# Third attention of a Flamingo-style kernel: its norms placed among residual rows, its groups turned into other banks, and eight tiles of scores ahead of group 2

## The chip, the cores and the metric

The kernel runs on one core of one Trainium2 chip. The metric is the device time of one execution in microseconds. TensorE (PE), VectorE (DVE), ScalarE (ACT), GpSimd (POOL) and SyncE (SP, which here only issues DMAs) each work through their own list of instructions in order. They meet at semaphores. Everything is float32 or a split of it in two parts.

## The reference, cut to what matters

Eight stages follow one another on `x` of 2 x 1024 tokens by 256: an attention and a feed-forward stage in each of four layers. Each stage normalizes `x`, computes, and adds its result, times a gate, to `x`.

```
x = x + tanh(g_ffn[1]) * ffn1(layernorm(x))              # dense: 8 experts, gated
x = x + tanh(g_xattn[2]) * attn2(layernorm(x), ctx)      # one head of 16, 64 keys
x = x + tanh(g_ffn[2]) * ffn2(layernorm(x))              # top-1 routing to 8 experts

attn2:  q = (x Wq) wq_h + bq_h;  k, v the same from ctx, 16 wide
        p = softmax(where(mask, -1e9, q k^T / 4))
        out = tile(p v, 16 times) Wo
ffn2:   logits = x router^T;  chosen = argmax;  rows gathered per expert, two matmuls
```

## The kernel before, in words

A tile is 128 tokens; there are 16 (`NT`), in four groups of four (`NG`, `GROUP`). `xs` holds `x`, `lnx` its normalized form, `xT` the transposed form that TensorE multiplies. The order of the work of every engine is written out by hand. The semaphores count: `x_done` residual rows, `ln_done` normalized tiles, `tr_done` transposed groups, `xt_done` copied groups.

A norm has four steps. `next_stats` takes the statistics of a tile behind its residual row (VectorE). `norm_moments` aggregates them for a group (VectorE). `norm_rstd` computes 1/sqrt on ScalarE (two instructions). `norm_group` writes four tiles of `lnx` (VectorE). TensorE then turns the group into two PSUM banks (`turn`) and ScalarE copies these into `xT` (`copy`).

**End of the second feed-forward stage (ffn1).** Its result lies transposed in `xT`; TensorE turns it back (`back`, L1050), two tiles to a bank in the order `BACK`, and VectorE adds the rows to `xs` (L2013) with `next_stats` (L1719) and `norm_moments` (L1694) between. Behind tiles 3 and 6 VectorE still adds up the last two blocks (`add_up`, L1947), for which the last turns back wait.

**Third attention (attn2).** TensorE first folds the weights (`wh`, into `wqkv`, copied by ScalarE at L1544), makes keys and values (banks 6 and 7) which VectorE takes over at L2245 and L2247, runs 24 multiplications whose result nobody reads (`fill`, L695), and turns group 0 and 1 (L1214). The order then is: queries of group 0 and 1, turns 2 and 3, scores of tiles 0 to 7, queries 2 and 3, six fills, the probabilities turned (L1238), scores of tiles 8 to 15, values. A query is a product of 16 x 512 that ScalarE copies with its bias (L1634). `bound` on VectorE (L2220 to L2225) masks the scores and subtracts their maximum, `exps` on ScalarE (L1643) exponentiates, `heads` on VectorE (L2232, L2235) divides and spreads the result over 128 columns. A loop over the 16 tiles follows: TensorE transposes a tile (L1272), ScalarE copies it (L1667), TensorE projects it, VectorE adds the row to `xs` (L2262), with `next_stats` and `norm_moments` between. Then come 40 fills.

**Third feed-forward stage (ffn2).** VectorE normalizes all four groups (`norm`, L1702) and computes the lower parts of the first weights (L2147). ScalarE, in this order: upper part of weight piece 0 (L1556), `norm_rstd` of group 3, pieces 1 to 3, and then the copies of the turned groups (L1579). TensorE turns the groups (L706) and multiplies them with the router (`logits_step`); VectorE takes the maxima from L2064 on and builds the row lists for the gathers.

Of the kernel before, what the change touches and what calls it, by code (L numbers as in the profile page):

```python
# [7 lines left out]
ALU = mybir.AluOpType  # L8
# [9 lines left out]
P = 128  # L18
# [3 lines left out]
NT = T // P  # L22
# [48 lines left out]
def build(nc, a, out, subs):  # L71
    with ExitStack() as ctx:
# [3 lines left out]
        def sem(name):  # L76
            return ctx.enter_context(nc.semaphore(name))
# [100 lines left out]
        with ExitStack() as a0_mem:  # L178
# [76 lines left out]
        a2_w, a2_wc, a2_kv, a2_kvb, a2_mask, a2_pool, in_a2 = (sem(f"a2_{n}") for n in ("w", "wc", "kv", "kvb", "mask", "pool", "in"))  # L255
        a2_q, a2_qc, a2_s, a2_min, a2_max, a2_sub, a2_exp, a2_ptr, a2_pt, a2_av, a2_rs, a2_oh, a2_tr, a2_ot, a2_proj = (
            sem(f"a2_{n}") for n in ("q", "qc", "s", "min", "max", "sub", "exp", "ptr", "pt", "av", "rs", "oh", "tr", "ot", "proj"))
        A2_Q, A2_S, A2_PTR, A2_AV, A2_TR, A2_PROJ = (4, 5, 4, 5), (6, 7), (0, 5), (1, 3), (0, 6), (1, 2)

        SLOT = {"11": 0, "12": 1, "21": 2, "22": 3}  # L260
# [425 lines left out]
        def _(pe):  # L686
# [5 lines left out]
            def fill(bank, count):  # L692

                for _ in range(count):
                    pe.matmul(ps[:, bank, 0:2 * P], filler[:, 0:P], filler, start=True, stop=True)  # L695
# [492 lines left out]
            def attn2(n):  # L1188
# [13 lines left out]
                    for k in range(KD):  # L1202
                        last = mm(ps[:, 6, b * HD:(b + 1) * HD], ctxD[:, k, b, :, :], wqkv[:, 2, k, :], k == 0, k == KD - 1)
                last.then_inc(a2_kv, 1)
                pe.wait_ge(x_done, NT * n - 2)
                fill(0, 24)

                def turn(g):
                    pe.wait_ge(ln_done, NT * n + GROUP * (g + 1))
                    if g >= 2:  # L1210
                        pe.wait_ge(xt_done, NG * n + g - 1)
                    for t in range(GROUP):
                        for k in range(KD):
                            last = pe.transpose(ps[:, g % 2 * 2 + k, t * P:(t + 1) * P],  # L1214
                                                lnx[:, g * GROUP + t, k * P:(k + 1) * P], ident[:, :])
                    last.then_inc(tr_done, 1)

                def query(g):
                    pe.wait_ge(xt_done, NG * n + g + 1)
                    if g >= 2:  # L1220
                        pe.wait_ge(a2_qc, g - 1)
                    for k in range(KD):
                        last = mm(ps[0:HD, A2_Q[g], :], wqkv[:, 0, k, :], xT[:, k, g * GT:(g + 1) * GT], k == 0, k == KD - 1)
                    last.then_inc(a2_q, 1)

                def scores(h):
                    pe.wait_ge(a2_qc, 2 * (h + 1))
                    pe.wait_ge(a2_kvb, 3)
                    for t in range(TB):
                        i = h * TB + t  # L1230
                        last = mm(ps[:, A2_S[h], t * S2:(t + 1) * S2], qhT[:, i * P:(i + 1) * P], khT[:, h, :], True, True)
                    last.then_inc(a2_s, 1)
# [14 lines left out]
                    last.then_inc(a2_av, 1)  # L1247

                turn(0)
                turn(1)  # L1250
                query(0)
                query(1)
                turn(2)
                turn(3)
                scores(0)
                query(2)
                query(3)
                fill(3, 6)
                turn_probs(0)
# [3 lines left out]
                for i in range(NT + 1):  # L1263
# [9 lines left out]
                    if i > 0:  # L1273
# [3 lines left out]
                        if i == 1:  # L1277
                            pe.wait_ge(a2_mask, 1)
                        mm(ps[:, A2_PROJ[(i - 1) % 2], 0:D], ot8[:, (i - 1) % 2, :], wo8[:, :], True, True).then_inc(a2_proj, 1)
                fill(7, 40)  # L1280

            if "attn2" in N:
                attn2(N["attn2"])
# [9 lines left out]
        def _(act):  # L1293
# [26 lines left out]
            def norm_rstd(n, g):  # L1320
                group_rstd(norm_no(n, g), g)
# [130 lines left out]
            def ffn1(n):  # L1452
# [87 lines left out]
                high(2 * UNITS - 1, "22")  # L1540
                high(2 * UNITS - 1, "21")
                act.preload_act_table_set("natural_log_exp_and_others")
                act.wait_ge(a2_w, 1)
                act.activation(wqkv[:, :, :, :], ps[:, 6, 0:3 * KD * HD].rearrange("p (i k j) -> p i k j", i=3, k=KD), ACT.Copy).then_inc(a2_wc, 1)  # L1544
                for g in range(NG):
                    norm_rstd(n + 1, g)

            def moe(layer, n):
                name = f"ffn{layer}"
# [81 lines left out]
            def attn2(n):  # L1631
                def query(g):
                    act.wait_ge(a2_q, g + 1)
                    act.activation(qhT[:, g * GT:(g + 1) * GT], ps[0:HD, A2_Q[g], :], ACT.Identity, bias=bh[:, 0:1]).then_inc(a2_qc, 1)  # L1634

                def copy(g):
                    act.wait_ge(tr_done, NG * n + g + 1)
                    act.activation(xT[:, :, g * GT:(g + 1) * GT], ps[:, g % 2 * 2:g % 2 * 2 + 2, :], ACT.Copy).then_inc(xt_done, 1)

                def exps(h):  # L1640
                    act.wait_ge(a2_sub, h + 1)
                    tiles = slice(h * TB, (h + 1) * TB)
                    act.activation(sc[:, 0, tiles, :], sc[:, 0, tiles, :], ACT.Exp).then_inc(a2_exp, 1)  # L1643

                def probs(h):
                    act.wait_ge(a2_ptr, h + 1)
                    act.activation(pt[:, h * PAIRS // 2:(h + 1) * PAIRS // 2, :], ps[:, A2_PTR[h], :].rearrange("p (q t) -> p q t", q=PAIRS // 2),
                                   ACT.Copy).then_inc(a2_pt, 1)
                copy(0)
                copy(1)  # L1650
                query(0)
                query(1)
                copy(2)
                copy(3)
                query(2)
                exps(0)
                query(3)
                probs(0)
                for i in range(NT):
                    if i == 1:  # L1660
                        exps(1)
                    if i == 2:
                        probs(1)
                    act.wait_ge(a2_tr, i + 1)
                    if i >= 2:
                        act.wait_ge(a2_proj, i - 1)
                    act.activation(ot8[:, i % 2, :], ps[:, A2_TR[i % 2], 0:P], ACT.Copy).then_inc(a2_ot, 1)  # L1667
                    if i in (7, 11, 15):
                        norm_rstd(n + 1, (i - 7) // 4)

            if "attn2" in N:
                attn2(N["attn2"])
# [9 lines left out]
        def _(dve):  # L1682
# [13 lines left out]
            def norm_moments(n, g):  # L1696
                moments(g, NT + 2 * GROUP * (g + 1) if n == 1 else NT * (n + 1) + GROUP * (g + 1))
# [113 lines left out]
            def mha(layer, m, n):  # L1811
# [89 lines left out]
                if soon:  # L1901
                    dve.wait_ge(ln_done, NT * (n + 1) + 3 * GROUP)
                    norm_group(n + 1, NG - 1)

            def ffn1(n):

                def x_sum(i, tp):
# [101 lines left out]
                for i in range(NT):  # L2009
                    if i in (3, 6):  # L2010
                        add_up(2 * UNITS - 1, 1, i // 6)
                    dve.wait_ge(f_back, i // 2 + 1)
                    dve.scalar_tensor_tensor(out=xs[:, i, :], in0=ps[:, BACK[i // 2], i % 2 * D:(i % 2 + 1) * D], scalar=gates[:, 5:6], in1=xs[:, i, :],  # L2013
                                             op0=ALU.mult, op1=ALU.add).then_inc(x_done, 1)
                    if i > 0:
                        next_stats(n, i - 1)
                    if i in (4, 8, 12):
                        norm_moments(n + 1, i // 4 - 1)
                next_stats(n, NT - 1)
                norm_moments(n + 1, NG - 1)  # L2020

# [116 lines left out]
            def moe(layer, n):  # L2138
                name = f"ffn{layer}"
                nth, cap, items, tiles = MOE.index(layer), CAP[layer], ITEMS[layer], IR[layer] // P  # L2140
                if layer:
                    norm(n)

                def weights_lower(*pieces):
# [72 lines left out]
            def attn2(n):  # L2217
# [10 lines left out]
                def heads(h):  # L2228
# [5 lines left out]
                    for r in range(2):  # L2234
# [1 line left out]
                                          av[:, r, :, 0:HD].unsqueeze(2).to_broadcast([P, half, HC, HD]),  # L2236
                                          rs2[:, r, h * half:(h + 1) * half].unsqueeze(2).unsqueeze(3).to_broadcast([P, half, HC, HD]),
                                          ALU.mult).then_inc(a2_oh, 1)
                dve.wait_ge(zeroed, 1 + 16 * 3)
                norm_group(n, 0)  # L2240
                norm_group(n, 1)
                dve.wait_ge(in_a2, 48)
                dve.wait_ge(a2_pool, 3)
                dve.wait_ge(a2_kv, 1)
                dve.tensor_scalar(khT[:, :, :], ps[0:HD, 7, 0:P].rearrange("p (b s) -> p b s", b=B), bh[:, 1:2], 0.25, ALU.add, ALU.mult).then_inc(a2_kvb, 1)  # L2245
                for b in range(B):
                    dve.tensor_tensor(vh[:, b, 0:HD], ps[:, 6, b * HD:(b + 1) * HD], bvh[:, :], ALU.add).then_inc(a2_kvb, 1)  # L2247
                norm_group(n, 2)
                norm_group(n, 3)
                dve.wait_ge(in_mask, 16 * MASKS[2])  # L2250
                link(dve.tensor_scalar(bmask[:, 0:TB, :], mask8[:, :, :], 0.0, BIG, ALU.is_equal, ALU.mult))
                link(dve.tensor_scalar(bmask[:, 0:TB, :], bmask[:, 0:TB, :], MASKED[2], None, ALU.add))
# [5 lines left out]
                for i in range(NT):  # L2258
                    if i == 4:
                        heads(1)  # L2260
                    dve.wait_ge(a2_proj, i + 1)
                    dve.scalar_tensor_tensor(out=xs[:, i, :], in0=ps[:, A2_PROJ[i % 2], 0:D], scalar=gates[:, 2:3], in1=xs[:, i, :],  # L2262
                                             op0=ALU.mult, op1=ALU.add).then_inc(x_done, 1)
                    if i > 0:
                        next_stats(n, i - 1)
                    if i in (4, 8, 12):
                        norm_moments(n + 1, i // 4 - 1)
                next_stats(n, NT - 1)
                norm_moments(n + 1, NG - 1)

# [54 lines left out]
```

## Time and profile before

| | |
|---|---|
| time, median of 3 runs | 1987.97 us (1986.66 to 1992.17) |
| the profiled execution's own time | 1972.97 us |
| its span in the trace | 1971.2 us |
| TensorE busy | 1848.1 us (94%) |
| VectorE busy | 1402.6 us (71%) |
| ScalarE busy | 1094.5 us (56%) |
| mean granted TensorE clock | 0.972 |

The change touches the stretch from about 1424 to 1497 us of the trace, which is 4% of the span. Times in rows are microseconds from the start of the span. A granted clock of 1.00 is TensorE at 2.4 GHz, 0.50 is 1.2 GHz; a value between them is a stretch that had both.

### The profile page before, as it was taken

What the parts mean: (1) busy time and instruction counts of PE and PEld (TensorE: products, weight loads), DVE (VectorE), ACT (ScalarE), POOL (GpSimd) and SP (SyncE); (2) the same over time, 40 slices, a digit from 0 to 9 for tenths busy, and PEclk for the clock granted to TensorE, in tenths of its full rate; (3) what the DMA queues carried; (4) which work ended last, traced back from release to release, by engine and by line L of the source; (5) the groups of instructions that cost most, each with busy time, mean ns of one, the idle gap of its engine ahead of it and who ended that gap; (6) DMA issues with size and microseconds to landing.
All of it is one profiled execution on the core that took longest, in us unless ns stands there. A gap on an engine that the chain in (4) does not pass through costs nothing.

```text
span 1971.2 us, 34855 instructions
## 1 busy us (share of the span) xinstructions
PE 1848.1 (94%) x11498; PEld 1557.3 (79%) x11498; DVE 1402.6 (71%) x2375; ACT 1094.5 (56%) x2003; POOL 730.8 (37%) x754
## 2 busy tenths in 40 slices
PE   7889996999999999999999999999998997898993
PEld 5579995877888888888888888888767997686993
DVE  4767777678777777777777777777766664866664
ACT  5548883685545555555555555455424774573771
POOL 6023331556434344353443534434002232342231
PEclk9999998999999999999999999999989999899997
DMA  4246662001000000100000000031114551203544
GB/s 126 71 144 200 200 176 76 2 17 33 17 32 16 32 32 16 32 16 32 32 16 32 21 27 32 16 116 50 30 38 150 147 147 50 71 2 118 176 138 142
DMA packets 113578, 138.95 MB, mean 70 GB/s; under 512 B 15332, under 2 KB 101606, under 8 KB 113504
## 3 DMA queue, kind: packets, MB, share of 16 engines
q1 hardware_dynamic: 105952, 121.70, 20.2%
q0 software_dynamic: 7552, 16.24, 2.8%
q8 instruction: 49, 0.80, 0.2%
q14 instruction: 25, 0.20, 0.0%
HBM read 117.22 MB, written 24.90 MB: 72 GB/s over the span
## 4 chain that ended last, share of the span: by engine, by line
PE 80%; DVE 10%; ACT 4%; issue 3%; DMA 2%; ACTq 0%; DVEq 0%; SPq 0%; POOL 0%; POOLq 0%
PE ps L688 43%; PE ps L949 10%; PE ps L950 10%; PE ps L951 10%; PE ps L695 2%; PE ps L882 1%; ACT ps L1595 1%; DVE xs L1799 1%; ACT wsplit L1556 1%; DVE bn L1719 1%; DVE wsplit L2180 1%; DVE lnx L1702 1%; PE ps L1149 1%; PE ps L1108 1%; DVE h_lo L2161 1%
## 5 line engine op out<-in xcount | busy, mean ns | idle before, releaser
L688 PE MATMUL ps<-h_hi,wsplit 128*128 128x512 f32 (+3 forms) x2016 | 588.5, 350 | 1.8 <-DVE xT L1947 1.3
L688 PEld LDWEIGHTS ps<-h_hi,wsplit 128*128 128x128 f32 x2016 | 366.7, 188 | 48.7 <-DVE xT L1947 1.8
L688 PE MATMUL ps<-h_lo,wsplit 128*128 128x512 f32 (+3 forms) x1008 | 352.5, 350 | 0.0
L574 POOL TENSOR_TENSOR wsplit<-wraw,zero 128x256 fp32r<-128x256 f32 (+2 forms) x160 | 150.9, 960 | 497.0 <-PE ps L951 407.7
L1477 ACT ACTIVATE lnx<-ps 128x512 f32<-128x512 f32 x384 | 229.3, 598 | 106.3 <-PE ps L951 63.6
L688 PE MATMUL ps<-xTh,wsplit 128*128 128x256 f32 (+2 forms) x992 | 254.9, 311 | 8.0 <-DVE h_lo L2161 4.4
L1486 ACT ACTIVATE h_act<-h_act 128x512 f32<-128x512 f32 x192 | 120.9, 629 | 211.8 <-DVE h_act L1925 211.7
L1947 DVE TENSOR_TENSOR xT<-xT,ps 128x1024 f32<-128x1024 f32 x124 | 151.3, 1220 | 117.7 <-PE ps L688 117.7
L1490 ACT ACTIVATE h_hi<-ps 128x512 fp32r<-128x512 f32 x256 | 152.6, 596 | 142.1 <-PE ps L688 139.8
L2161 DVE TENSOR_TENSOR h_lo<-ps,h_hi 128x256 fp32r<-128x256 f32 (+2 forms) x248 | 117.7, 475 | 151.3 <-ACT h_hi L1599 150.1
L1934 DVE TENSOR_TENSOR ps<-h_act,ps 128x512 f32<-128x512 f32 x256 | 177.4, 693 | 44.3 <-PE ps L951 30.2
L688 PEld LDWEIGHTS ps<-h_lo,wsplit 128*128 128x128 f32 x1008 | 189.5, 188 | 22.7
L949 PE MATMUL ps<-xTh,wsplit 128*128 128x512 f32 x512 | 203.1, 397 | 0.7 <-DVE xTl L1917 0.4
L950 PE MATMUL ps<-xTl,wsplit 128*128 128x512 f32 x512 | 202.5, 396 | 0.0
L951 PE MATMUL ps<-xTh,wsplit 128*128 128x512 f32 x512 | 202.5, 395 | 0.0
L635 POOL DMA_INDIRECT y_tok<-xT,y_idx x78 | 87.9, 1126 | 297.3 <-DVE xT L2176 283.0
L688 PEld LDWEIGHTS ps<-xTh,wsplit 128*128 128x128 f32 x992 | 174.6, 188 | 16.0 <-DVE h_lo L2161 12.2
L1595 ACT ACTIVATE ps<-ps,b1c 128x256 f32<-128x256 f32 (+2 forms) x248 | 120.7, 487 | 101.6 <-PE ps L688 100.5
L1925 DVE TENSOR_TENSOR h_act<-ps,lnx 128x512 f32<-128x512 f32 x192 | 132.5, 690 | 61.8 <-PE ps L951 61.6
L1938 DVE TENSOR_TENSOR h_lo<-ps,h_hi 128x512 fp32r<-128x512 f32 x256 | 174.5, 682 | 0.0
L628 POOL DMA_INDIRECT xT<-x_tok,x_idx x78 | 91.5, 1173 | 199.7 <-DVE x_idx L2120 173.2
L949 PE MATMUL ps<-wsplit 128*128 128x512 f32 x384 | 151.0, 393 | 2.9 <-DVE ps L1925 1.5
(289 smaller groups left out, 3580.3 us busy)
## 6 DMA issues: line engine op xcount, KB each, us to landing
wraw<-in_L_w SPq DMA_DIRECT2D x124, 512.0 KB, 3.9
wraw<-in_L_ffn_Wg SPq DMA_DIRECT2D x32, 256.0 KB, 2.7
wraw<-in_L_ffn_Wu SPq DMA_DIRECT2D x32, 256.0 KB, 3.0
wraw<-in_L_ffn_Wd SPq DMA_DIRECT2D x32, 256.0 KB, 3.6
x_tok<-lnx SPq DMA_DIRECT2D x12, 512.0 KB, 4.1
lnx<-y_tok SPq DMA_DIRECT2D x12, 512.0 KB, 5.9
y_tok<-lnx SPq DMA_DIRECT2D x3, 2048.0 KB, 13.8
wat<-in_attn SPq DMA_DIRECT2D x16, 256.0 KB, 4.8
```

The lines of the kernel that those rows point to most:

```text
L574: return pool.tensor_tensor(out_, in_, zero[:, :].to_broadcast(shape), ALU.add)
L688: return pe.matmul(out_, lhsT, rhs, start=start, stop=stop)
L949: pe.matmul(o, w_hi, x_hi, start=fresh, stop=False, skip_group_check=True)
L950: pe.matmul(o, w_hi, x_lo, start=False, stop=False, skip_group_check=True)
L951: pe.matmul(o, w_lo, x_hi, start=False, stop=True, skip_group_check=True).then_inc(p_early if m == 0 and i in (2, 5) else p_up, 1)
L1477: act.activation(dst, ps[:, 3 * m + (1 if i == 2 else 2), :], ACT.Copy).then_inc(p_copy, 1)
L1490: act.activation(h_hi[:, SLOT[c], :], ps[:, H_BANK[c], :], ACT.Copy).then_inc(p_hi, 1)
L1595: act.activation(ps[:, f % 2, 0:cap], ps[:, f % 2, 0:cap], func, bias=b1c[:, layer, bass.ds(ex * FC + f, 1)]).then_inc(m_act, 1)
L1934: dve.tensor_tensor(bank, h_act[:, c in ("12", "21"), :], bank, ALU.mult).then_inc(p_h, 1)
L1938: dve.tensor_tensor(h_lo[:, SLOT[c], :], ps[:, H_BANK[c], :], h_hi[:, SLOT[c], :].bitcast(F32), ALU.subtract).then_inc(p_lo, 1)
L1947: dve.tensor_tensor(xT[:, :, blk], xT[:, :, blk], ps[:, 6:8, :], ALU.add).then_inc(p_y, 1)
L2161: dve.tensor_tensor(h_lo[:, f % 4, 0:cap], ps[:, f % 2, 0:cap], h_hi[:, f % 4, 0:cap].bitcast(F32), ALU.subtract).then_inc(f_lo, 1)
```

## The change

- `norm_group` of attn2's groups 0, 1 and 2 moves from behind all 16 residual rows of ffn1 to behind rows 5, 10 and 14. VectorE's take-over of keys and values moves to row 12 (`keys_of_attn2`). ScalarE computes `norm_rstd` of groups 0 and 1 ahead of the copy of the folded weights, that of group 3 behind attn2's second copy.
- The groups are turned into banks 4-5, 6-7, 0-1 and 2-3. Groups 0, 2 and 3 wait for the residual rows that empty these banks, group 1 for the keys and values.
- TensorE's wait for ffn1's rows and the 24 fills ahead of the first turn go.
- TensorE's order is now turn 0, query 0, turn 1, query 1, scores of tiles 0 to 7, turn 2, query 2, turn 3, query 3. ScalarE's follows it, and `exps(0)` stands ahead of the copy of group 3.
- `norm_group` of ffn2's groups 0, 1 and 2 moves into attn2's residual loop, behind rows 7, 11 and 15, with their `norm_rstd` one tile earlier on ScalarE. Only group 3 is normalized behind the loop.
- The 40 fills behind the loop become 10 and a wait for the last residual row.

```
+        A2_TURN = (4, 6, 0, 2)
...
-                pe.wait_ge(x_done, NT * n - 2)
-                fill(0, 24)
                 def turn(g):
                     pe.wait_ge(ln_done, NT * n + GROUP * (g + 1))
-                    if g >= 2:
-                        pe.wait_ge(xt_done, NG * n + g - 1)
+                    if g == 1:
+                        pe.wait_ge(a2_kvb, 3)
+                    else:
+                        pe.wait_ge(x_done, NT * (n - 1) + {0: 10, 2: 14, 3: 16}[g])
...
                 turn(0)
+                query(0)
                 turn(1)
-                query(0)
                 query(1)
+                scores(0)
                 turn(2)
+                query(2)
                 turn(3)
-                scores(0)
-                query(2)
                 query(3)
...
-                fill(7, 40)
+                fill(7, 10)
+                pe.wait_ge(x_done, NT * (n + 1))
...
+                norm_rstd(n + 1, 0)
+                norm_rstd(n + 1, 1)
                 act.wait_ge(a2_w, 1)
                 act.activation(wqkv[:, :, :, :], ...).then_inc(a2_wc, 1)
-                for g in range(NG):
-                    norm_rstd(n + 1, g)
+                norm_rstd(n + 1, 2)
...
                 copy(0)
+                query(0)
                 copy(1)
-                query(0)
+                norm_rstd(n, NG - 1)
                 query(1)
                 copy(2)
-                copy(3)
                 query(2)
                 exps(0)
+                copy(3)
                 query(3)
...
-                    if i in (7, 11, 15):
-                        norm_rstd(n + 1, (i - 7) // 4)
+                    if i in (6, 10, 14):
+                        norm_rstd(n + 1, (i - 6) // 4)
...
+            def keys_of_attn2():
+                dve.wait_ge(in_a2, 48)
+                dve.wait_ge(a2_pool, 3)
+                dve.wait_ge(a2_kv, 1)
+                dve.tensor_scalar(khT[:, :, :], ...).then_inc(a2_kvb, 1)
+                for b in range(B):
+                    dve.tensor_tensor(vh[:, b, 0:HD], ...).then_inc(a2_kvb, 1)
...
+                    if i == 5:
+                        dve.wait_ge(zeroed, 1 + 16 * 3)
+                    if i == 12:
+                        keys_of_attn2()
+                    if i in (5, 10, 14):
+                        norm_group(n + 1, (5, 10, 14).index(i))
...
-                if layer:
+                if layer == 2:
+                    norm_group(n, NG - 1)
+                elif layer == 3:
                     norm(n)
...
+                    if i in (7, 11, 15):
+                        norm_group(n + 1, i // 4 - 1)
```

## Rows read from the trace of the kernel before

**Rows 1.** The page: busy time, share and instructions of each engine.
```profile
PE 1848.1 (94%) x11498; PEld 1557.3 (79%) x11498; DVE 1402.6 (71%) x2375; ACT 1094.5 (56%) x2003; POOL 730.8 (37%) x754
```

**Rows 2.** Chain that ended last, 1415 to 1515: start, us, what.
```profile
1440.98 4.04 PE ps L695 x24
1445.03 0.89 PE ps L1214 x8
1445.94 1.03 ACT xT L1638
1447.02 3.61 PE ps L688 x8
...
1471.84 0.21 PE ps L1272
1472.06 0.87 PE ps L688 x2
...
1481.74 0.38 DVE xs L2262
1482.12 0.34 DVE bn L1719
1482.49 0.38 DVE mv L1694 x4
```

**Rows 3.** Stages: length, busy PE, PEld, DVE, ACT, POOL, granted clock, DMA.
```profile
1434.70:1440.80 6.10, 5.76 (x38) 5.12 (x37) 6.03 (x24) 1.54 (x7) 0.00 (x0) 0.68 0.00 1
1440.80:1445.00 4.20, 4.20 (x27) 3.23 (x28) 4.17 (x17) 0.50 (x2) 0.00 (x0) 0.65 0.00 0
1445.00:1449.00 4.00, 3.76 (x22) 2.04 (x21) 3.75 (x14) 1.99 (x3) 0.00 (x0) 1.00 0.00 0
...
1470.00:1474.60 4.60, 4.60 (x18) 3.60 (x19) 2.44 (x7) 1.11 (x4) 0.00 (x0) 0.51 0.02 5
...
1478.00:1484.00 6.00, 5.21 (x23) 2.98 (x22) 5.93 (x24) 3.12 (x11) 0.00 (x0) 1.00 0.00 0
```

**Rows 4.** Timeline of PE: start, us, work, idle time ahead.
```profile
1450.56 1.97 PE L1214 MATMUL ps<-ident,lnx 128*128 128x128 f32 x16
1452.45 1.99 PE L688 MATMUL ps<-khT,qhT 16*128 16x64 f32 x16
...
1457.91 0.83 PE L695 MATMUL ps<-ident 128*128 128x256 bf16 x6
...
1459.11 1.99 PE L688 MATMUL ps<-khT,qhT 16*128 16x64 f32 x16
...
1483.89 4.53 PE L695 MATMUL ps<-ident 128*128 128x256 bf16 x40
1488.26 1.91 PE L706 MATMUL ps<-ident,lnx 128*128 128x128 f32 x16
1490.50 0.65 PE L688 MATMUL ps<-xT,wr 128*32 128x128 f32 x16 [0.33 <-ACT xT L1579]
```

**Rows 5.** Timeline of DVE, the same columns.
```profile
1432.49 1.22 DVE L1947 TENSOR_TENSOR xT<-xT,ps 128x1024 f32<-128x1024 f32 x1 [0.58 <-PE ps L688]
...
1442.36 2.65 DVE L1702 TENSOR_SCALAR lnx<-xs,mv,st_rstd 128x256 f32<-128x256 f32 x8
...
1485.67 5.23 DVE L1702 TENSOR_SCALAR lnx<-xs,mv,st_rstd 128x256 f32<-128x256 f32 x16
...
1496.69 0.29 DVE L2064 TENSOR_REDUCE r_m<-ps 128x16 f32<-128x128 f32 x1 [3.53 <-PE ps L739]
```

**Rows 6.** Timeline of ACT, the same columns.
```profile
1456.30 0.68 ACT L1634 ACTIVATE qhT<-ps,bh 16x512 f32<-16x512 f32 x1 [2.68 <-PE ps L688]
1456.89 0.61 ACT L1643 ACTIVATE sc<-sc 128x512 f32<-128x512 f32 x1
...
1485.78 0.30 ACT L1316 ACTIVATE st_std<-mv,eps 128x4 f32<-128x4 f32 x1 [1.39 <-DVE mv L1694]
1486.22 2.94 ACT L1556 ACTIVATE wsplit<-wraw 128x1024 fp32r<-128x1024 f32 x3
```

More of the change, by code:

```diff
@@ L1204, in attn2 @@
                 last.then_inc(a2_kv, 1)
-                pe.wait_ge(x_done, NT * n - 2)
-                fill(0, 24)
                 def turn(g):
                     pe.wait_ge(ln_done, NT * n + GROUP * (g + 1))
-                    if g >= 2:
-                        pe.wait_ge(xt_done, NG * n + g - 1)
+                    if g == 1:
+                        pe.wait_ge(a2_kvb, 3)
+                    else:
+                        pe.wait_ge(x_done, NT * (n - 1) + {0: 10, 2: 14, 3: 16}[g])
                     for t in range(GROUP):
                         for k in range(KD):
-                            last = pe.transpose(ps[:, g % 2 * 2 + k, t * P:(t + 1) * P],
+                            last = pe.transpose(ps[:, A2_TURN[g] + k, t * P:(t + 1) * P],
                                                 lnx[:, g * GROUP + t, k * P:(k + 1) * P], ident[:, :])
@@ L1637, in copy @@
                     act.wait_ge(tr_done, NG * n + g + 1)
-                    act.activation(xT[:, :, g * GT:(g + 1) * GT], ps[:, g % 2 * 2:g % 2 * 2 + 2, :], ACT.Copy).then_inc(xt_done, 1)
+                    act.activation(xT[:, :, g * GT:(g + 1) * GT], ps[:, A2_TURN[g]:A2_TURN[g] + KD, :], ACT.Copy).then_inc(xt_done, 1)
                 def exps(h):
@@ L1903, in mha @@
                     norm_group(n + 1, NG - 1)
+            def keys_of_attn2():
+                dve.wait_ge(in_a2, 48)
+                dve.wait_ge(a2_pool, 3)
+                dve.wait_ge(a2_kv, 1)
+                dve.tensor_scalar(khT[:, :, :], ps[0:HD, 7, 0:P].rearrange("p (b s) -> p b s", b=B), bh[:, 1:2], 0.25, ALU.add, ALU.mult).then_inc(a2_kvb, 1)
+                for b in range(B):
+                    dve.tensor_tensor(vh[:, b, 0:HD], ps[:, 6, b * HD:(b + 1) * HD], bvh[:, :], ALU.add).then_inc(a2_kvb, 1)
             def ffn1(n):
@@ L2238, in heads @@
                                           ALU.mult).then_inc(a2_oh, 1)
[L2239 to L2249, printed above, removed]
+                norm_group(n, NG - 1)
                 dve.wait_ge(in_mask, 16 * MASKS[2])
```

## The prediction

> **What bounds the kernel now.** I read the page first: TensorE is busy for 94% of the span, VectorE for 71%, ScalarE for 56% [rows 1]. That is a mean over eight stages, and the change touches 4% of the span. So I read the chain of waits from 1415 to 1515 next, to see which engine ends each stretch, then the table of stages for the granted clock, and last the timelines of the three engines for durations and the idle time ahead of each group.
>
> The chain shows four stretches. (A) To 1445.03 it runs through 24 fills, 4.04 us, which cover VectorE's last rows and the first norms [rows 2, 5]. (B) From 1445.03 to the second scores at 1459.11 TensorE works almost without a gap: turn 0, a copy of 1.03 us behind which turn 1 is hidden, four queries, turns 2 and 3 without idle time ahead, scores [rows 2, 4]. (C) In attn2's residual loop TensorE bounds the first rows, at half clock and 1.08 us a row (0.21 + 0.87) [rows 2]; from row 4 on, at full clock, VectorE does, at 0.72 us a row (0.38 + 0.34) and 0.38 us of moments for four rows, and is busy 5.93 of 6.00 us [rows 2, 3]. (D) Behind the loop ScalarE decides: `norm_rstd` of group 3 (from 1485.78) has to wait for VectorE's last moments, three weight pieces of 2.94 us stand behind it, and only then come the copies of the turned groups. The turns at 1488.26 came just in time, and the maxima of the routing at 1496.69 [rows 4, 5, 6].
>
> **A, the early start.** Behind row 5 VectorE idles 0.58 us until `add_up` at 1432.49 [rows 5]. `norm_group(0)` is put there. Four tiles cost 4 x 0.33 = 1.3 us (5.23 us for 16) [rows 5], so 0.75 us of it is not hidden, and add_up, the last eight turns back, the folding and the keys' product on TensorE come 0.75 us later. The other norms among ffn1's rows only change places with norms behind them: no cost, as turn 0 needs group 0 alone. Keys and values at row 12 can be ready at about 1441.7, when VectorE gets there: nothing either. Turn 0 now stands right behind the keys' product, so it starts at 1440.98 + 0.75 = 1441.7 instead of 1445.03. **Gain 3.3 us.**
>
> **B, the order.** The work of TensorE is the same; what lies beside it is not. Before, from the first turn to the second scores: 1459.11 - 1445.03 = 14.1 us. After, each group is turned, copied and multiplied before the next may be turned. One such cycle is turn and copy, 1447.02 - 1445.03 = 2.0 us, and a query of 1.8 us (3.61 for two) [rows 2]: four cycles, 15.2 us. The first scores wait for ScalarE's copy of query 1 (0.68 us, and some 0.2 us of handing over) [rows 6] and take 1.9 us (the row's 1.99 less what overlaps with the next work) [rows 4]: 2.8 us. `exps(0)`, 0.61 us and not startable before query 2 is copied, stands ahead of the copy of group 3 [rows 6]: 0.5 us. Fills and turned probabilities, 1459.11 - 1457.91 = 1.2 us [rows 4]. Sum 19.7 us, so **loss 5.6 us**; against the 3.3 us of A, a net loss of 2.3 us at full clock. The third `norm_rstd`, which stands behind copy 1, is two instructions of 0.3 us in ScalarE's free time; behind it are the norm of group 3 and the mask, which VectorE finishes before the scores arrive.
>
> The clock comes on top. TensorE fell to half clock around 1437, while it was busy 5.76 of 6.10 us with the small matmuls of the folding, and was back at 1.00 in the row from 1445 on, behind 3 us of dense fills at half clock [rows 3]. After the change there are no fills, and a copy's gap of 1.1 us stands between turn and query. I take the clock to stay at half over turn 0 (0.9 us more, from 1.97 for two at full clock), query 0 (1.8) and turn 1 (0.9) [rows 2, 4]: **loss 3.6 us**. Bounds: 0 if it is back at once, and 4 x (0.9 + 1.8) = 10.8 us if it stays at half through the four groups. I take the lower part since a query alone is 3.6 us of unbroken work at half clock, nearly as much as the fills that brought it back.
>
> That the change uses all eight banks is the point on which a page speaks for it: the Trainium skill, Perfetto Trace Analysis, Matmul Optimizations, asks to leverage all eight banks for parallelism, and Optimizing Tensor Performance there wants independent groups rotated through banks so that one's evacuation overlaps the next's matmuls. This trace has turn 2 at 1450.56 [rows 4], long after the bank's copy was done (1445.94 + 1.03 = 1446.97) and with no idle time ahead of it, so by the row the new banks are worth 0 in the order that stands now; what the rule would give is among the rivals.
>
> **C, the norms in the loop.** Twelve tiles, 12 x 0.33 = **4.0 us**, go in front of VectorE's last moments, in rows in which VectorE is the bound (5.93 of 6.00) [rows 3, 5]. Behind the loop the same 4.0 us leave VectorE, but there it is not awaited: it idled 3.53 us before the maxima [rows 5]. ScalarE's `norm_rstd(3)`, the three pieces and the copies all move back by 4.0 us [rows 6]. Taking 30 of the 40 fills away (1488.26 - 1483.89 = 4.4 us for 40) gains nothing, because the copies wait for ScalarE and not for the turns. ScalarE's one earlier `norm_rstd` may hold up one tile's copy for some tenths; bound 0.3 us, taken as 0. The half-clock stretch on the first rows I take to recur: the same wait for `heads(0)` and the same small value matmuls are ahead of it.
>
> **D, the clock in the routing.** TensorE turns groups 0 and 1 right behind the last row, and then waits for the copy of group 0, that is 0.5 us of `norm_rstd` + 2.94 + 1.0 us less those turns, over 3 us idle where fills stood [rows 6]. Its chain to 1496.69 has four router products of 0.65 and two turns of 0.9 between copies, with turns of logits and fills some 5 us of 6.2 (1496.69 - 1490.50) [rows 4, 5]. At half clock for half of it: **2.3 us**; bounds 0 and 5.
>
> **DMAs and queues.** SP's four stores of `lnx` wait for `ln_done` and now go out earlier for three groups, the last about as late as the norm of group 3; they are done before the row lists. GpSimd's gathers wait for the lists. No cost.
>
> **Sum.** -3.3 + 5.6 + 3.6 + 4.0 + 2.3 = **+12 us**. The profiled execution took 1972.97 us around a span of 1971.2; the changed span would be 1983. That execution lies 15 us under the median of the runs, so I put the difference to the median: 1988 + 12 = **2000 us**, its own range 1995 to 2004. About 0.3% (6 us) is what a measurement of this kernel can tell from no change.
>
> **Rivals.**
> 1. *The clock is back early.* Neither B's nor D's half clock appears, and the stretch on the loop's first rows shrinks too, which gives back up to 8 rows' difference of 0.36 us (1.08 - 0.72), 2.9 us. For it: the clock was 1.00 over most of this region [rows 3]. -3.3 + 5.6 + 4.0 - 2.9 = +3.4: **1991**. Chance 0.17.
> 2. *Half clock throughout B*, and all of D: 7.2 us over my B, 2.7 over my D, together at most +22; in the middle of that +17: **2005**. For it: a gap at every group. Against: TensorE is still busy most of the time. Chance 0.18.
> 3. *Not slower: half clock in the loop hides the norms.* Where TensorE runs at half clock in all rows, four rows take it 4 x 1.08 = 4.3 us, and VectorE with norms needs 4 x 0.72 + 0.38 + 1.3 = 4.6 us. The norms then cost 3 x 0.3 = 0.9 instead of 4.0 us, and cutting the 30 fills turns the groups some 2 us sooner. In A and B the 24 fills that go are worth 24/40 of 8.8 us, 5.3 us at half clock, and the first turn starts that much sooner, which about cancels B's 5.6 us. The 30 fills of C count from the last projection, which the copies then wait for. Sum -1: **1987**. It decides once the half clock lasts past row 8; against it, this trace has it end by row 4 [rows 3]. Chance 0.08.
> 4. *Copies overlap as by the rule on banks.* If turn g+1 ran while g is copied, B's 5.6 us would shrink to 0.7, and A's gain would stay: -3.3 + 0.7 + 4.0 = +1.4: **1989**. Against it: the order written out has each query ahead of the next turn, and TensorE works in order. By the Trainium skill's two sections named above this is what the banks are for. Chance 0.04.
>
> The forecast has 0.53. The range 1988 to 2006 leaves out rival 3, the outer part of rival 2 and chance in the median of the runs, under 2 in 10 in all. Slower by over 0.3%: the forecast but its lowest part (0.50), rival 2 (0.18) and a tail of rival 1 (0.05), 0.73. Within 0.3%: 0.20. Faster: 0.07, from rival 3 with a longer slow stretch.
>
> **What would show it.** Turn 0 near 1441.7 and the first scores no earlier than before; gaps of about 1.1 us ahead of every query; `oh` of group 0 two to seven us later than before; 12 norm tiles inside the loop with no idle time of VectorE around them; `norm_rstd(3)` directly behind the loop and three weight pieces ahead of the first copy; a granted clock of 0.5 somewhere before the first scores and again in the routing. Wrong would make it: a clock that stays at 1.00 in both places, or a loop bound by TensorE, which would hide the norms.

## The result and the profile after

The changed kernel takes 1999.65 us (median of 9 runs, 1994.38 to 2002.47), the kernel before 1984.84 us in the same series. The ratio is 1.0072, with a 95% interval of 1.0059 to 1.0085: 14.3 us slower, 11.7 to 16.9 by the interval. The forecast was 2000 us, 12 us slower.

The two profiled executions have spans of 1971.2 and 1999.4 us. Of these 28 us, 3.5 lie ahead of the mark named below, 12.4 in the stretch of the change and 12.3 behind it. The last part isn't the change's: behind the maxima of the routing the kernel before takes 474.5 us, the changed kernel 486.8 in this execution and 474.9 in the other that was profiled (changed_again, below). So all readings below count from one mark that both kernels have, the last pair of `h_lo` of the feed-forward stage. In the kernel before it is this line of the chain (start, us, what):

```profile
1423.64 1.34 DVE h_lo L1938 x2
```

The chain of the changed kernel over the same stretch:

```profile
1427.18 1.34 DVE h_lo L1949 x2
...
1435.42 1.38 DVE lnx L1705 x4
1436.80 1.14 DVE xT L1958
1437.99 1.09 PE ps L1051 x8
...
1445.93 1.80 PE ps L1214 x8
1447.75 1.03 ACT xT L1640
1448.83 3.59 PE ps L689 x4
1452.42 1.82 PE ps L1214 x8
1454.27 1.03 ACT xT L1640
1455.35 1.91 PE ps L689 x4
1457.28 0.69 ACT qhT L1636
1458.01 1.99 PE ps L689 x16
1460.00 1.09 PE ps L1214 x8
1461.11 1.03 ACT xT L1640
1462.19 3.59 PE ps L689 x4
1465.78 1.91 PE ps L1214 x8
1467.72 1.03 ACT xT L1640
1468.80 1.89 PE ps L689 x4
...
1471.88 1.94 PE ps L689 x16
```

The reader is to see two things in it. Every turn (L1214), its copy (L1640) and its query (L689 x4) stand one behind the other, four times; in the chain before there was one copy on this way [rows 2]. And the same piece of work has two lengths: a query is 3.59 us or 1.9 us, a turn 1.8 to 1.9 or 1.09 us. The table of stages names the reason. Its columns are the length, the busy time of PE, PEld, DVE, ACT and POOL, the granted clock, and DMA:

```profile
1447.60:1452.30 4.70, 3.59 (x5) 0.43 (x4) 3.13 (x13) 1.02 (x1) 0.00 (x0) 0.50 0.00 0
1452.40:1455.00 2.60, 1.83 (x9) 1.52 (x8) 0.00 (x0) 1.41 (x2) 0.00 (x0) 0.69 0.00 0
1461.00:1466.00 5.00, 3.89 (x7) 0.71 (x7) 1.55 (x3) 1.20 (x2) 0.00 (x0) 0.50 0.02 3
```

Query 0 and query 2 ran at half clock. TensorE fell to it in the small matmuls of the folding as before [rows 3], and a second time after it had come back. In all six profiled executions with this order and no fills in its pauses, queries 0 and 2 take 3.27 to 3.60 us and queries 1 and 3 1.89.

The loop, on VectorE's timeline (start, us, work, idle time ahead and who ended it):

```profile
1489.32 0.48 DVE L2271 SCALAR_TENSOR_TENSOR xs<-ps,gates,xs 128x256 f32<-128x256 f32 x1 [0.60 <-PE ps L689]
...
1490.05 1.36 DVE L1705 TENSOR_SCALAR lnx<-xs,mv,st_rstd 128x256 f32<-128x256 f32 x4
...
1494.82 1.37 DVE L1705 TENSOR_SCALAR lnx<-xs,mv,st_rstd 128x256 f32<-128x256 f32 x4
...
1499.14 0.48 DVE L2271 SCALAR_TENSOR_TENSOR xs<-ps,gates,xs 128x256 f32<-128x256 f32 x1 [0.39 <-PE ps L689]
...
1501.61 0.38 DVE L1697 BATCH_NORM_AGGREGATE mv<-bn 128x2 f32<-128x6 f32 x4
1502.59 1.38 DVE L1705 TENSOR_SCALAR lnx<-xs,mv,st_rstd 128x256 f32<-128x256 f32 x4 [0.60 <-ACT st_rstd L1319]
...
1512.64 0.29 DVE L2081 TENSOR_REDUCE r_m<-ps 128x16 f32<-128x128 f32 x1 [6.40 <-PE ps L740]
```

and behind it on ScalarE's:

```profile
1502.02 0.30 ACT L1317 ACTIVATE st_std<-mv,eps 128x4 f32<-128x4 f32 x1 [3.02 <-DVE mv L1697]
...
1502.46 2.93 ACT L1558 ACTIVATE wsplit<-wraw 128x1024 fp32r<-128x1024 f32 x3
1505.30 1.92 ACT L1581 ACTIVATE xT<-ps 128x1024 f32<-128x1024 f32 x2
```

VectorE does the norms between the rows and has some 1 us of idle time in all around them; then ScalarE, which waited 3.02 us for the last moments, runs the three weight pieces, and VectorE idles 6.40 us before the maxima (3.53 before [rows 5]). All marks, in microseconds behind the last `h_lo` pair (before: 1423.64; after: 1427.18):

| mark | before | after | difference | step |
|---|---|---|---|---|
| turn 0 in the chain | 21.39 | 18.75 | -2.6 | -2.6 |
| `oh` of tiles 0 to 7 | 39.79 | 48.96 | +9.2 | +11.8 |
| residual row 4 | 51.5 | 58.9 | +7.4 | -1.8 |
| last moments | 61.73 | 74.43 | +12.7 | +5.3 |
| maxima of the routing | 73.05 | 85.46 | +12.4 | -0.3 |

So 12.4 us of the difference lie in this stretch. The 1.8 us that the changed kernel gains on the loop's first rows are not the change's: from `oh` of tiles 0 to 7 to that of tiles 8 to 15 (`heads(1)`) nine of the thirteen profiled executions take 8.5 to 8.9 us and four 10.5 us. The kernel before is among the four, and so is the changed kernel in changed_again.

### The profile page after: what moved, and what is told of

The parts are those of the page before. It is cut to its first block, busy times and chain, and to the rows that moved or that the text cites. A ratio compares the mean times of both kernels' runs of the same rounds, so it can differ in the third digit from the quotient of the medians.

```text
span 1999.4 us, 34750 instructions
## 1 busy us (share of the span) xinstructions
PE 1852.0 (93%) x11444; PEld 1555.8 (78%) x11444; DVE 1403.7 (70%) x2375; ACT 1094.6 (55%) x2003; POOL 732.6 (37%) x754
## 4 chain that ended last, share of the span: by engine, by line
PE 79%; DVE 10%; ACT 5%; issue 3%; DMA 2%; another core or an unknown queue 1%; ACTq 0%; SPq 0%; POOL 0%; DVEq 0%; POOLq 0%
PE ps L689 43%; PE ps L950 10%; PE ps L951 10%; PE ps L952 10%; PE ps L883 1%; PE ps L696 1%; ACT ps L1597 1%; DVE lnx L1705 1%; ACT wsplit L1558 1%; DVE bn L1722 1%; DVE xs L1802 1%; PE ps L1109 1%; PE ps L1150 1%; ACT h_hi L1601 1%; DVE h_lo L2180 1%
## 5 line engine op out<-in xcount | busy, mean ns | idle before, releaser
L689 PE MATMUL ps<-h_hi,wsplit 128*128 128x512 f32 (+3 forms) x2016 | 589.8, 350 | 1.8 <-DVE xT L1958 1.3
L689 PEld LDWEIGHTS ps<-h_hi,wsplit 128*128 128x128 f32 x2016 | 367.8, 189 | 48.7 <-DVE xT L1958 1.8
L689 PE MATMUL ps<-h_lo,wsplit 128*128 128x512 f32 (+3 forms) x1008 | 353.2, 350 | 0.0
L689 PE MATMUL ps<-xTh,wsplit 128*128 128x256 f32 (+2 forms) x992 | 257.0, 313 | 19.1 <-DVE h_lo L2180 15.1
L689 PEld LDWEIGHTS ps<-h_lo,wsplit 128*128 128x128 f32 x1008 | 190.1, 189 | 22.7
L689 PEld LDWEIGHTS ps<-xTh,wsplit 128*128 128x128 f32 x992 | 175.6, 189 | 27.9 <-DVE h_lo L2180 22.9
```

The costliest lines, as they stand in the source:

```text
L689: return pe.matmul(out_, lhsT, rhs, start=start, stop=stop)
```

## The experiments

All times are against the kernel before, run beside each kernel on the same chip; 1973 us is its median there, so 0.1% is 2.0 us. "Front" is the place of `oh` of tiles 0 to 7 behind the last `h_lo` pair, 39.79 us before and 48.96 after.

**loop_undone: the norms of the loop put back.**

```
-                fill(7, 10)
-                pe.wait_ge(x_done, NT * (n + 1))
+                fill(7, 40)
...
-                    if i in (6, 10, 14):
-                        norm_rstd(n + 1, (i - 6) // 4)
+                    if i in (7, 11, 15):
+                        norm_rstd(n + 1, (i - 7) // 4)
...
-                if layer == 2:
-                    norm_group(n, NG - 1)
-                elif layer == 3:
+                if layer:
                     norm(n)
...
-                    if i in (7, 11, 15):
-                        norm_group(n + 1, i // 4 - 1)
```

> The changed kernel with its third attention's residual loop, what stands behind it and the 40 fills as they were before; the front half of the change stays. Theory (VectorE bounds the loop, so 12 norm tiles of 0.33 us in it are paid in full): 4 to 5 us faster than the changed kernel, that is 9 to 10 us slower than the kernel before, with the last moments about 5 us earlier behind the loop's first row. Rival (the norms are hidden behind TensorE, the whole loss is in the front half): still 13 to 15 us slower than before.

Measured: 1.0044 (1.0032 to 1.0055), 8.7 us slower than before, where 9 to 10 were expected. The front lies at 48.85 us as in the changed kernel; from `heads(1)` to the last moments it takes 12.19 us instead of 16.74, 4.6 us less. The norms were not hidden. (The kernel before takes 11.46 us with the same instructions; here TensorE ran three projections at 1.06 to 1.19 us, half clock, and VectorE waited 0.5 us for them.)

**loop_only: the mirror image,** the kernel before with only the lines above added.

> The kernel before with nothing but the norms in the third attention's residual loop, one ScalarE pair a tile earlier, and 10 fills and a wait in place of 40. Theory (VectorE bounds the loop): 4 to 5 us slower than before. Rival (half clock on TensorE hides the norms, or the clock falls in the routing behind it): 0 to 1 us if hidden, 7 us or more if the clock falls.

Measured: 1.0026 (1.0014 to 1.0037), 5.1 us slower, at the upper end of the 4 to 5 us expected. These 5.1 us are not the norms alone. From `oh` of tiles 0 to 7 to the last moments this kernel takes 25.08 us; loop_undone, which has the same short first rows and the old loop, takes 21.00, so the loop costs 4.1 us. Another 1.0 us lies in the routing behind it (12.32 us from the last moments to the maxima, 11.32 before). The two halves add: 0.26% and 0.44% make 0.70%, the whole is 0.72%. The chain in the loop of this kernel:

```profile
1474.41 1.28 DVE lnx L1703 x4
1475.69 0.39 DVE xs L2265
1476.08 0.34 DVE bn L1720
1476.45 0.39 DVE mv L1695 x4
1476.86 0.30 ACT st_std L1317
1477.30 0.27 ACT ot L1668
1477.61 0.71 PE ps L688 x2
1478.35 0.48 DVE xs L2265
```

It shows something that the forecast had at nothing: the pair of `norm_rstd`, one tile earlier, stands in ScalarE's list ahead of the copy of the next tile (`ot`). It waits for the moments, the copy waits for it, TensorE's projection for the copy, and VectorE's row for that. How long VectorE then waits depends on the clock. Here the projection takes 0.71 us and VectorE idles 0.1 us. At the first pair of the same loop, and of the changed kernel's loop, TensorE is at or near half clock (PE's timelines, loop_only first, then the changed kernel):

```profile
1472.52 1.03 PE L688 MATMUL ps<-wo,ot 128*128 128x256 f32 x2 [0.61 <-ACT ot L1668]
1488.08 1.19 PE L689 MATMUL ps<-wo,ot 128*128 128x256 f32 x2 [0.61 <-ACT ot L1670]
```

VectorE idles 0.44 us behind the first and 0.60 us behind the second.

**old_order: the new banks and early norms with the old order** of turns, copies, queries and scores.

```
                 turn(0)
-                query(0)
                 turn(1)
+                query(0)
                 query(1)
-                scores(0)
                 turn(2)
-                query(2)
                 turn(3)
+                scores(0)
+                query(2)
                 query(3)
```

(and ScalarE's list to match.)

> The changed kernel with the order of the third attention's turns, copies, queries and scores as before (turn 0, turn 1, query 0, query 1, turn 2, turn 3, scores, query 2, query 3), but with the new banks, the early norms, no fills ahead of turn 0, and the norms in the loop. Theory (the loss in front comes from turn, copy and query standing in a row): the front now gains its 2.6 us, the loop loses 4 to 5: 1 to 3 us slower than before, about 12 us faster than the changed kernel. Rival (the loss in front comes from the 24 fills that are gone, which leave TensorE at half clock): the clock stays at half over the first turns and queries, 7 us or more slower than before.

Measured: 1.0014 (1.0005 to 1.0022), 2.8 us slower than before, within the theory's 1 to 3, and so some 11 to 12 us faster than the changed kernel. The order is the larger part of the loss. TensorE's timeline:

```profile
1442.88 3.65 PE L1214 MATMUL ps<-ident,lnx 128*128 128x128 f32 x16
1446.47 4.46 PE L689 MATMUL ps<-xT,wqkv 128*16 128x512 f32 x8
1450.86 1.97 PE L1214 MATMUL ps<-ident,lnx 128*128 128x128 f32 x16
```

and the table of stages over it, with the granted clock behind POOL's column (0.50, 0.97):

```profile
1442.00:1448.00 6.00, 6.00 (x23) 4.42 (x24) 5.05 (x23) 2.64 (x5) 0.00 (x0) 0.50 0.00 0
1448.00:1452.00 4.00, 4.00 (x17) 1.67 (x16) 2.15 (x6) 1.77 (x5) 0.00 (x0) 0.97 0.00 0
```

The first two turns take 3.65 us at half clock, where they took less than two at full clock [rows 4]. Turn 0 starts 2.9 us earlier than before, and the front is at 39.18 us, only 0.6 us earlier. The clock took back most of what the early start had given, but TensorE is busy without a gap, and the level was 0.97 from 1448 on and stayed up; the fall did not come twice, as it did in the changed kernel.

**gap_fills: the changed kernel with its waits filled.**

```
                 turn(0)
+                fill(0, 10)
                 query(0)
                 turn(1)
+                fill(0, 10)
                 query(1)
+                fill(0, 7)
                 scores(0)
                 turn(2)
+                fill(3, 10)
                 query(2)
                 turn(3)
+                fill(0, 10)
                 query(3)
```

> The changed kernel with fills of 0.107 us that nobody reads in the five waits of TensorE's new order: 10 between each turn and its query, 7 ahead of the first scores. The waits stay as long, only the clock can change. Theory (about 3 us of the front's loss are waits net of the early start, and about 6 us are half clock): 8 to 10 us slower than before, 5 to 6 us faster than the changed kernel, with the clock at 1.00 from the second query on. Rival (all of the front's loss is waiting, the half clock costs nothing because copies are waited for anyway): as the changed kernel, 14 to 15 us slower than before.

Measured: 1.0040 (1.0028 to 1.0053), 7.9 us slower than before. That is 0.1 us better than the 8 to 10 that were expected. Its order and its waits are those of the changed kernel, its front is at 45.25 us instead of 48.96.

```profile
1450.00:1458.00 8.00, 7.98 (x52) 5.11 (x51) 2.51 (x7) 2.77 (x5) 0.00 (x0) 1.00 0.01 2
1458.00:1466.00 8.00, 7.91 (x46) 4.08 (x44) 2.04 (x4) 3.45 (x5) 0.00 (x0) 1.00 0.00 0
```

Multiplications that nobody reads made the kernel faster: with them the granted clock is 1.00 from 1450 on and every later query takes 1.89 us. The 5.5 us by which the front is still late are the waits and the half clock on the first turn and query, and 1.0 us of it is the experiment's own: at half clock the ten fills behind turn 0 took 2.13 us and kept query 0 waiting, where the pause was 1.1.

**no_fills: the kernel before without its 24 fills.** `fill(0, 24)` goes, nothing else.

> The kernel before without the 24 fills ahead of the first turn; nothing else. Theory (the fills bring the clock back, and the first turn waits for VectorE's norm anyway): the first turn starts 1 us earlier, but turns and queries run at half clock for longer; 1 to 4 us slower than before. Rival (fills are no more than 4 us of work in front of the first turn): 1 us faster than before, with the clock back as before.

Measured: 1.0011 (1.0001 to 1.0021), 2.2 us slower. In the trace the first turn stands 1.0 us earlier, both turns take 3.65 us together, and the front is at 40.30, 0.5 us later. That is the theory's side, at its lower end (by the interval 0.2 to 4.1 us): taken alone, the fills save little more than they cost.

**early_norms: the front of the change in the old order, with the loop as before.**

> The front half of the change with the order of turns, copies, queries and scores as before, and the loop and all behind it as before. Theory (the two halves add): old_order's +2.8 us less loop_only's +5.1 us, so 1 to 3 us faster than before; the second scores lie 0.6 us earlier behind the end of the feed-forward stage. Rival (the early start is worth its full 2.9 us at the loop): 3 to 5 us faster.

Measured: 0.9998 (0.9985 to 1.0010), no difference, though its profiled front was at 37.76 us, 2.0 us earlier. The 1 to 3 us expected were not found; the interval reaches from 3.0 us faster to 2.0 slower and doesn't rule them out. Nor is the profiled front a fixed size: old_order and best, with the same front, have it at 39.18 and 39.20, with turn 0 at 18.5 us instead of 17.7 and the first two queries at 4.4 us instead of 3.9.

**weights_first: ScalarE's last `norm_rstd` behind the four weight pieces,** in the changed kernel.

```
                     weights_upper(0, 0, 0)
-                    norm_rstd(n, NG - 1)
+                    if layer == 3:
+                        norm_rstd(n, NG - 1)
                     for q in range(1, 4):
                         weights_upper(0, 0, q)
+                    if layer == 2:
+                        norm_rstd(n, NG - 1)
```

> The changed kernel with ScalarE's third and last norm_rstd of the stage behind its four weight pieces instead of behind the first. Theory (behind the loop ScalarE decides: norm_rstd of group 3, three pieces of 2.9 us, then the copies): the copies come 2.4 to 2.9 us earlier, so 12 us slower than before instead of 14 to 15. Rival (TensorE and the last norm decide): as the changed kernel.

Measured: 1.0044 (1.0030 to 1.0059), 8.7 us slower than before, where 12 were expected. In the trace ScalarE's four pieces now lie in the time in which it waited for the last moments:

```profile
1495.88 3.88 ACT L1558 ACTIVATE wsplit<-wraw 128x1024 fp32r<-128x1024 f32 x4
1499.66 0.29 ACT L1317 ACTIVATE st_std<-mv,eps 128x4 f32<-128x4 f32 x1
...
1500.40 1.94 ACT L1584 ACTIVATE xT<-ps 128x1024 f32<-128x1024 f32 x2 [0.21 <-PE ps L707]
```

From the last moments to the maxima it takes 8.53 us instead of 11.03. That explains 2.5 us; the rest of the difference to the changed kernel's 14.3 us was measured on another chip, and changed_again and weights_first_2 below put the two side by side.

**best: early_norms, weights_first and 28 fills for 40.**

> early_norms with norm_rstd of group 3 behind the four weight pieces and 28 fills instead of 40 behind the loop, so that the first turn of the routing stands when its norm is ready. Theory (ScalarE's three pieces and the fills hold up the first copy): 1 us earlier than in early_norms at the maxima of the routing, 2 to 4 us faster than before in all. Rival (the 40 fills and the pieces lie beside VectorE's norms and hide each other): as early_norms.

Measured: 0.9996 (0.9985 to 1.0007), no difference from the kernel before; the 2 to 4 us expected were not found, though 2 us would lie in the interval. Behind the last moments it is 10.21 us to the maxima, 1.1 us less than before, as expected, but neither this nor the front's gain can be told in the timed runs. No version here beats the kernel before by more than the measurement can tell.

**changed_again, weights_first_2 and rstd_late, side by side on one chip.**

> The changed kernel once more, on the chip on which the next two run. Theory (its loss is that of the stretch): 12 to 15 us slower than before. Rival (part of the 15 us first measured is the first chip's own): 9 to 12 us slower.

Measured: 1.0075 (1.0060 to 1.0090); the loss is not the first chip's own. In this execution the routing was slower than in the first one:

```profile
1499.28 1.08 PE L689 MATMUL ps<-xT,wr 128*32 128x128 f32 x16 [2.85 <-ACT xT L1581]
1500.29 1.97 PE L707 MATMUL ps<-ident,lnx 128*128 128x128 f32 x8
1502.19 0.68 PE L689 MATMUL ps<-xT,wr 128*32 128x128 f32 x16
```

TensorE idles for 2.85 us, and the router product and the turn behind it take 1.08 and 1.97 us, where the next product takes 0.68 and the next turn 1.04. From the last moments to the maxima it is 12.39 us here.

> The changed kernel with the last norm_rstd behind the four weight pieces, once more, beside the changed kernel on the same chip. Theory: 3 us faster than the changed kernel, as the traces say. Rival: no difference, the 5 us between their ratios to the kernel before being the two chips' own.

Measured: 1.0047 (1.0034 to 1.0060), median 1983.25 us against 1986.65 us of changed_again: 3.4 us, as the theory said, with 5 and 6 runs and intervals that just touch. The traces have 8.46 us against 12.39 between last moments and maxima, 3.9 us.

> The changed kernel with the three norm_rstd of the loop behind tiles 7, 11 and 15 as before, instead of 6, 10 and 14. Theory (ScalarE waits for VectorE's moments while the next tile's copy stands behind it, which leaves VectorE idle some 0.2 to 0.6 us three times): the loop is 0.5 to 1.2 us shorter in the trace, too little for the timed runs. Rival (the later pair holds up the norms themselves): the loop is as long or longer.

```
-                    if i in (6, 10, 14):
-                        norm_rstd(n + 1, (i - 6) // 4)
+                    if i in (7, 11, 15):
+                        norm_rstd(n + 1, (i - 7) // 4)
```

Measured: 1.0061 (1.0046 to 1.0075), which overlaps with changed_again. From `heads(1)` to the last moments it takes 15.67 us against 16.16 to 16.88 in the seven traces of kernels with the early pair and the norms in the loop. The sign is that of the theory, the size 0.5 to 1.2 us; since the clock in the loop differs between these executions, it isn't settled. At like length of the projection it is smaller: behind one of 1.10 us VectorE idles 0.23 us here, behind one of 1.11 us with the early pair (old_order) 0.51.

## Why the prediction was right

The sum of +12 us stands beside 12.4 us in the stretch of the first profile, 13.4 in that of changed_again, and 14.3 and 14.8 us in the runs. Its terms stand like this:

| term | predicted | first profile | changed_again |
|---|---|---|---|
| A, the early start of turn 0 | -3.3 | -2.6 | -3.2 |
| B, turn, copy and query in a row | +5.6 | +6.2 | +6.1 |
| B, half clock on turns and queries | +3.6 | +5.6 | +4.7 |
| C, the loop | +4.0 | +3.5 (+5.3 and -1.8) | +4.7 |
| D, half clock in the routing | +2.3 | -0.3 | +1.1 |

The mechanisms were right: waits in a row, half clock on top of them, norms paid in the loop. That the sum came within half a microsecond of the first profile is partly luck, for the clock's term in B was 2.0 us too small and that in D 2.6 us too large. It is luck too that 2000 us stands beside 1999.65: the forecast added 12 us to 1988, while the kernel before took 1984.84 in the series with the result, and the medians differ by 14.8.

**A.** The hole of 0.58 us took the norm as worked out: `add_up` followed it at once, and the last turns back came 10.81 us behind the mark instead of 10.13, 0.7 us later. The start was 0.7 us later than predicted because more of the folding ran at half clock (3.67 us in the chain, 2.94 before).

**B, the waits.** The chain takes 25.95 us from the first turn (1445.93) to the second scores (1471.88), 11.8 us more than before. At full clock the same chain has a turn at 1.09 and a query at 1.9 us, so that turn 0, query 0, turn 1, query 2 and turn 3 would have been 0.7, 1.7, 0.7, 1.7 and 0.8 us shorter: 5.6 us. The remaining 6.2 us are waits and handovers: about 1.1 us of idle TensorE ahead of each query, 0.8 ahead of the first scores, and the ends of turns and queries that no longer lie beside the next piece. The prediction took a cycle of turn, copy and query at 3.8 us, from pieces of the old order that overlap their neighbours; alone and at full clock it is 2.2 us to the query's start (1460.00 to 1462.19) and 1.9 for the query, 4.1, which makes 1.1 us in four cycles. Against that, the 0.5 us for `exps(0)` ahead of the copy of group 3 did not come: turn 3, at half clock, ended at 1467.70, after `exps`, and the copy began at once (1467.72). old_order shows that these two terms together hang on the order: with it back, everything else as in the change, the front is 9.8 us earlier.

**B, the clock.** This term was mis-sized. The prediction let TensorE fall once and come back behind query 0, since a query at half clock is long unbroken work. It did come back, and its three pieces cost 3.1 us, but the pauses of 1.1 us went on, and it fell again for query 2 and turn 3, another 2.5 us. gap_fills shows the size that hangs on the pauses: 3.7 us of the front. What remains, at the first turn and query, is in old_order and no_fills too, where there are no pauses: it comes from the folding and the missing fills.

**C.** The mechanism and 4.0 us for the twelve tiles held. Compared among executions whose first rows take equally long, the loop with the norms costs 4.1 us (loop_only against loop_undone) to 4.7 us (changed_again against the kernel before). Two things were not in the sum. ScalarE's earlier pair held up the next tile's copy; the prediction put that at 0 with a bound of 0.3, and VectorE idled 1.1 us in this loop. Over the seven traces that wait is 0.1 us where the projection behind it takes 0.70 us, and 0.3 to 0.6 us where it takes 0.91 to 1.22, because TensorE is at half clock again. loop_undone, with neither the early pair nor the norms in the loop, has 0.5 us of such waits, so about half of the 1.1 us is the clock's alone. And the slow first rows ended sooner in this execution (row 4 came 9.9 us behind `oh` and not 11.7). In other executions they do not: changed_again, early_norms and no_fills have 10.5 us from `oh` to `heads(1)`, as before, where the changed kernel has 8.7.

**D.** ScalarE's pieces between the last moments and the copies decide, as weights_first shows by 2.5 us of the trace and weights_first_2 by 3.4 us of the runs. In both traces the first router product runs at 0.64 us, behind a wait of 0.3 us and not of 3. The half clock after TensorE's idle time comes in some executions and not in others. Of six profiled ones with the norms in the loop and ScalarE's order as in the change, four take 12.3 to 12.4 us from the last moments to the maxima (changed_again, loop_only, gap_fills, rstd_late) and two 11.0 us (the changed kernel, old_order); the kernel before takes 11.3. The four with the 40 fills (before, loop_undone, no_fills, early_norms), in which TensorE waits some 0.3 us there, all take 11.3. No run changes these fills alone. So half clock, where it came, cost 1.3 to 1.4 us, and the term is at most +1.1 us against the kernel before, half of the forecast: the level was back by the second router product, before most of the work of the routing. (By its own terms the prediction would have had 2.5, half of 5 us, and not 2.3.)

**The rivals.** That the clock is back early was not so. Nor did half clock last throughout B: queries 1 and 3 are at full clock in all six executions. That half clock in the loop hides the norms did not happen: in loop_only three projections behind the first moments run at 1.03 to 1.06 us, and the norms are paid all the same; half clock in all rows, which that rival asked for, came in no run. The rival on banks is refuted by the chain: turn 1 stands behind query 0 each time, whatever bank it has. By the Trainium skill, Perfetto Trace Analysis, Matmul Optimizations, all eight banks should be used for parallelism. In this order the trace shows nothing gained by it; in old_order turn 1 runs beside the copy of group 0 with the new banks as it did with the old ones. No run changes the banks alone, so what they are worth by themselves isn't measured.

**Left open.** The runs show 14.3 and 14.8 us (ratios 1.0072 and 1.0075), the stretch of the first profile 12.4. In changed_again the stretch is 13.4 us longer than before (86.47 against 73.05). The last microsecond or two are not located. In the ten other runs the stretch of the one profile and the timed difference agree within 2.1 us. Why the first profiled execution of the changed kernel took 12 us more behind the stretch is open.

## What to carry to other kernels

An early start of one engine was worth nothing here that the runs could tell: count how many handovers to another engine then stand in a row, and keep two units of work in flight, so that the copy of one lies beside the transposes of the next. Before moving work "into a loop", ask which engine ends each row of it; work moved ahead of the last instruction of an engine that bounds the loop is paid in full, and what waits behind that instruction on a third engine moves back with it. Pauses of a microsecond between TensorE's pieces cost twice if the clock falls on top of them, so price a pause with the work around it at both levels.

## What the runs showed of the hardware

The granted clock fell to 0.50 with pauses of only 1.1 us between pieces of work (query 2 at 3.59 us; at 3.42 to 3.60 us in all six executions), and rose to 1.00 and stayed there, in the one execution profiled, when the same pauses were filled with 128x256 multiplications (1.09 us for ten). The same instructions in the same order had the falls at different places from one execution to the next: `oh` of tiles 0 to 7 lies at 48.96 and 47.44 us in two executions of the changed kernel, and at 39.18, 37.76 and 39.20 us in three kernels with the same front (old_order, early_norms, best). A single profile of such a stretch is therefore uncertain by 1 to 2 us, as much as what early_norms and best were meant to gain.
